# Routing made ready during attention, top-2 choice per batch, and identity products between the logits

## The chip, the cores and the metric

The kernel runs on one core of one Trainium2 chip. Its time is device microseconds (us) of one execution. The kernel before the change takes 1905.55 us, the median of 3 runs (1905.47 to 1907.82).

## The reference, cut to what matters

Four blocks add to a residual `x` of 4 batches x 1024 tokens x 256 channels: attention over a context, a mixture of experts, a second attention, and a second mixture of experts. What the change touches is the routing of both mixtures:

```python
x = x + attention0(layernorm(x), ctx)
x = x + ffn0(layernorm(x))        # 8 experts, hidden 1024, top 2
x = x + attention1(layernorm(x), ctx)
x = x + ffn1(layernorm(x))        # 8 experts, hidden 512, top 2
# in each ffn:
logits = z @ router               # z: normalised tokens, 8 logits per token
probs = softmax(logits)
top_w, top_idx = top_k(probs, 2)
w = top_w / (sum(top_w) + 1e-9)
out = sum over the 2 chosen experts of w * expert(z)
```

The reference computes all experts for every token; the kernel computes only the two chosen ones, so it must first sort the 8192 (token, choice) pairs by expert.

## The kernel before, in words

A token tile is 128 tokens, one per partition; there are T = 32 tiles, TB = 8 per batch. The program is a row of blocks, each with one instruction stream per engine; a block starts on all engines when all of them have ended the one before. The order is written out by hand: every engine runs its list in order and waits on counters. The blocks are `attention0_inputs`, `attention0`, `route` (layer 0), `experts` (layer 0), `attention1_context`, `attention1`, `route` (layer 1), `experts` (layer 1).

`route` (line 800) has three stages.

1. **The turning loop.** `summarise` (line 306) turns the per-token sums that attention left in `g.stats` into mean and variance for all 32 tiles, on DVE; POOL raises the variance to the power -1/2 (line 877), 4 columns first and then 28. DVE's `center` (line 972) writes the normalised tile into one of R = 4 slots of `z`. PE transposes it in two halves (`turn`, line 896), ACT copies the result to SBUF (`copy_out`, line 932) and writes a float16 copy of z (`token_high`, line 937), DVE the float16 remainder (`token_low`, line 977), which frees the slot. PE multiplies the transposed tile with the 8-column router weight `gw` (`logits`, line 902). SP stores the halves to `token_parts` in DRAM batch by batch, and between them brings five experts' weights (`bring_home`). `gw` itself is loaded at the start of the block, and PE waits for it before its first instruction (line 889).
2. **The choice.** After the last tile DVE works on all 32 tiles x 8 experts = 256 columns: each instruction increments `v_step` and DVE waits for it (`step`, line 994). It copies the logits, finds the best and the second best expert (lines 1005 to 1012), adds the two one-hot rows (line 1014); PE multiplies that with a strictly upper triangular matrix (ranks inside a tile, line 915) and with ones (totals of each tile, line 916); DVE runs 8 prefix sums over the tiles (line 1028) and computes each pair's slot, lane and block. ACT's exponentials (line 943) give the shares.
3. **The inverse permutation.** For 8 sets of 8 columns DVE builds one-hot rows of the block times token and times share (`same_block`, line 1072, then lines 1084 and 1086), and ACT (lines 953, 959; even sets) or DVE (line 1075; odd sets) the one-hot rows of the lane; PE multiplies them (line 923, 8 float32 products of 156 columns a set, two records each in the trace) and sums in one PSUM bank. `block_hot` and `lane_hot` have two buffers. In the loop from line 1079 DVE issues `same_block(i + 1)` before the two products of set i; `same_block(n)` waits until PE has read set n - 2.

At the end the slots' tokens and weights are read from PSUM (lines 1093, 1094), and `experts` starts by gathering rows from `token_parts`.

In `attention1` (line 1509) body c of each engine works on tile c in a pipeline: POOL's two passes over the 128x1232 scores (lines 1696, 1700), PE's transposes of them (line 1601), DVE's sums; the last batch drains over six bodies.

## Time and profile before

| | |
|---|---|
| median of 3 runs | 1905.55 us (1905.47 to 1907.82) |
| the profiled execution's own time | 1910.07 us |
| its span, first to last instruction | 1908.4 us |
| mean granted TensorE clock | 0.909 of full |
| PE / PEld busy | 1610.3 us (84%) / 1188.1 us (62%) |
| DVE / ACT / POOL busy | 1101.4 (58%) / 854.0 (45%) / 712.3 us (37%) |
| DMA | mean 84 GB/s |
| `route`, layer 0 | 573.5 to 690.9 us of the span |
| `route`, layer 1 | 1422.8 to 1538.8 us of the span |

PE is the matmul engine and PEld its weight loads. A busy share is an average over stages that have different limits. The granted clock is 1.00 at 2.4 GHz and 0.50 at 1.2 GHz. The times of the rows further down are counted from the span's first instruction. In the views by time, a bracket at the end of a row gives the engine's idle time before it and what ended that.

### The profile page before, as it was taken

The page shows a single profiled execution, that of the slowest core. Times are in us where ns is not written, and L with a number is a line of the kernel's source. Part 1 is how long each engine was busy: PE and PEld are TensorE (multiplying, and loading weights), DVE is VectorE, ACT ScalarE, POOL GpSimd, SP SyncE. Part 2 cuts the span into 40 slices and gives each one's busy share as a digit, 9 for nine tenths or more (in the row PEclk, how much of TensorE's full clock was granted, in tenths as well). Part 3 has the DMA queues.
Part 4 walks back from the last instruction along what each step waited for, and adds up shares of the span by engine and source line. Part 5 has one row for each costly group of instructions (what it writes and reads, how often), then busy time and mean ns, then how long its engine had stood idle before and what let it go on. Part 6 is the DMA issues. An engine that isn't in the chain of part 4 may idle for free. (4 is left out here: it accounts for less than half of the span.)

```text
span 1908.4 us, 38766 instructions
## 1 busy us (share of the span) xinstructions
PE 1610.3 (84%) x12456; PEld 1188.1 (62%) x12457; DVE 1101.4 (58%) x1819; ACT 854.0 (45%) x1506; POOL 712.3 (37%) x515
## 2 busy tenths in 40 slices
PE   4798898897987369999999994899968479999997
PEld 1433434334337358888888882677757468888886
DVE  4677677687676524445554431788857434444443
ACT  1663755655634215555554440466744312222221
POOL 2401302104001014655555441577760025556554
PEclk9899899899895679999999996799995689999999
DMA  4321320412307134555553221200016043333333
GB/s 127 105 67 45 110 66 25 129 44 77 100 22 271 59 141 128 141 140 135 132 132 66 47 42 37 83 24 22 24 56 221 0 133 59 62 56 58 63 55 45
DMA packets 104310, 159.84 MB, mean 84 GB/s; under 512 B 10810, under 2 KB 69998, under 8 KB 104110
## 3 DMA queue, kind: packets, MB, share of 16 engines
q1 hardware_dynamic: 73007, 117.52, 19.0%
q0 software_dynamic: 29952, 40.91, 12.3%
q8 instruction: 43, 0.70, 0.1%
q10 hardware_dynamic: 1279, 0.46, 0.1%
q14 instruction: 29, 0.24, 0.0%
HBM read 91.49 MB, written 67.37 MB: 83 GB/s over the span
## 5 line engine op out<-in xcount | busy, mean ns | idle before, releaser
L1234 PE MATMUL e_ph<-e_zTt,weights_a 128*128 128x256 f16 x3744 | 424.6, 274 | 32.5 <-issue 28.3
L1234 PEld LDWEIGHTS e_ph<-e_zTt,weights_a 128*128 x3744 | 360.6, 98 | 96.1 <-issue 53.1
L1188 POOL DMA_INDIRECT e_zt<-token_parts,slot_token x156 | 167.1, 1071 | 271.4 <-issue 263.4
L1319 ACT ACTIVATE e_h<-e_ph,e_b 128x256 f32<-128x256 f32 x312 | 131.0, 471 | 240.0 <-PE e_ph L1234 162.6
L1367 DVE TENSOR_TENSOR e_hl<-e_h,e_hh 128x512 f16<-128x512 f32 x156 | 104.7, 692 | 226.7 <-ACT e_hh L1333 202.1
L1198 POOL DMA_INDIRECT token_rows<-e_ysb,slot_token x78 | 151.7, 1945 | 200.1 <-DVE e_ysb L1384 185.7
L1248 PE MATMUL e_pyt<-weights_b,e_hh 128*128 x1248 | 210.7, 273 | 1.1 <-DVE e_ysb L1384 1.1
L640 ACT ACTIVATE probs<-lower_banks,shift 128x1024 f32<-128x1024 f32 x128 | 137.7, 1111 | 118.8 <-PE lower_banks L500 113.8
L1198 POOL DMA_INDIRECT out_dram<-e_ysb,slot_token x78 | 124.5, 1596 | 133.9 <-DVE e_ysb L1388 110.5
L1248 PE MATMUL e_pyt<-weights_b,e_hl 128*128 x624 | 170.1, 273 | 0.0
L1358 DVE SCALAR_TENSOR_TENSOR e_g<-e_ph,e_h 128x512 f32<-128x512 f32 x78 | 54.0, 692 | 178.1 <-PE e_ph L1234 171.3
L660 DVE TENSOR_TENSOR acc<-acc,probs 128x1024 f32<-128x1024 f32 (+1 forms) x112 | 136.9, 1222 | 28.3 <-ACT probs L640 25.2
L511 PE MATMUL middle_banks<-probs,v 128*64 128x512 f32 (+1 forms) x576 | 142.6, 606 | 1.0 <-ACT probs L640 1.0
L500 PE MATMUL lower_banks<-qT,kT 128*128 128x512 f16 x512 | 131.2, 401 | 4.7 <-ACT kT L606 4.7
L1248 PEld LDWEIGHTS e_pyt<-weights_b,e_hh 128*128 128x128 f16 x1248 | 122.1, 98 | 15.1 <-issue 1.3
L1322 ACT ACTIVATE e_h<-e_ph 128x512 f32<-128x512 f32 x78 | 46.6, 598 | 170.5 <-PE e_ph L1234 159.6
L923 PE MATMUL e_pinv<-e_block_hot,e_lane_hot 128*128 128x156 f32 x256 | 61.5, 425 | 64.2 <-DVE e_block_hot L1086 64.2
L500 PEld LDWEIGHTS lower_banks<-qT,kT 128*128 128x128 f16 x512 | 46.8, 102 | 106.2 <-issue 33.4
L1248 PE MATMUL e_pyt<-weights,e_hh 128*128 x624 | 108.6, 273 | 0.5 <-DVE e_ysb L1388 0.5
L676 POOL COPY cshift<-shift 77x1 f32 x4 | 0.7, 184 | 278.2 <-PE middle_banks L468 278.2
L923 PEld LDWEIGHTS e_pinv<-e_block_hot,e_lane_hot 128*128 128x128 f32 x256 | 57.8, 295 | 68.9 <-issue 68.9
L1333 ACT CAST e_hh<-e_h 128x512 f16<-128x512 f32 x156 | 92.4, 620 | 0.0
(240 smaller groups left out, 2973.0 us busy)
## 6 DMA issues: line engine op xcount, KB each, us to landing
weight_parts<-w_split SPq DMA_DIRECT2D x32, 512.0 KB, 3.3
weights_a<-weight_parts SPq DMA_DIRECT2D x16, 1024.0 KB
x_sb<-in_u SPq DMA_DIRECT2D x24, 512.0 KB
weight_parts<-x_sb SPq DMA_DIRECT2D x24, 512.0 KB
w_raw<-in_w1T SPq DMA_DIRECT2D x16, 512.0 KB, 4.4
w_raw<-in_w2T SPq DMA_DIRECT2D x16, 512.0 KB, 4.7
weights_b<-weight_parts SPq DMA_DIRECT2D x8, 1024.0 KB
token_parts<-x_sb SPq DMA_DIRECT2D x8, 1024.0 KB, 5.3
```

The source lines that it names most:

```text
L500: last = pe.matmul(sc[0:rows(k), n % 2, j, :], kk, q, start=(form == 0), stop=(form == 1))
L511: last = pe.matmul(po[u % 2][j * HD0:(j + 1) * HD0, :], v[0:rows(k), k, h * HD0:(h + 1) * HD0], pr[0:rows(k), n % 4, j, :], start=(k == 0) ...
L640: act.activation(pr[0:r, n % 4], sc[0:r, n % 2], ACT.Exp, bias=bias).then_inc(e_done, 1)
L660: dve.tensor_tensor(acc[0:r, u % 2], acc[0:r, u % 2], pr[0:r, n % 4], ALU.add).then_inc(acc_done, 1)
L923: pe.matmul(pinv[:, 0:2 * NT * C], lane_hot[n % 2][:, w, :], block_hot[n % 2][:, w].rearrange("p h n -> p (h n)"), start=(c == 0), stop=(c ...
L1188: pool.indirect_dma_start(zt[:, i % 2, c, :], None, g.zrows, at).then_inc(ld[i % 2], 16)
L1198: pool.indirect_dma_start(g.rows[layer], at, ysb[:, s, c, :], None, compute_op=ALU.add).then_inc(sto[s], 16)
L1234: last = pe.matmul(ph[:, q, f, :], up_w(wp, e, k, 2 * q + f), zTs[:, s, 2 * zp + k, :], start=(n == 0), stop=(n == 5))
L1248: last = pe.matmul(py[c][:, 0, :], hp[:, s, f, c * P:(c + 1) * P], down_w(wp, e, f), start=(n == 0), stop=(n == 3 * NF - 1))
L1319: last = act.activation(h32[:, q % 2, f, :], ph[:, q, f, :], ACT.Relu, bias=b1[:, bass.ds(e, 1), 2 * q + f], scale=1.0 / WS)
L1333: act.copy(hh[:, s, 2 * q:2 * q + 2, :], src[:, q % 2]).then_inc(hi_done, 1)
L1367: dve.tensor_tensor(hl[:, s, 2 * q:2 * q + 2, :], src[:, q % 2], hh[:, s, 2 * q:2 * q + 2, :], ALU.subtract).then_inc(lo_done, 1)
```

## The change

- `gw` for both layers is loaded in `attention0` (`g.gw`); `route` no longer loads it or waits for it.
- The temporaries of `summarise` are shared, and it takes a range of tiles and a run number. Tiles 0 to 23 (LAST = 24) are summarised on DVE, and rooted on POOL by the new `roots`, inside the attentions: in `attention0` in the last batch after its projections, in `attention1` in body c = 15. `route` does tiles 24 to 31 only: DVE after its second `token_low`, POOL at the block's start, and DVE waits for that before `center(24)`.
- The choice is made batch by batch (`choose(b)`, 64 columns): for batches 0, 1, 2 inside the turning loop after `center` at t = 10, 18, 26, with ACT's exponentials at t = 12, 20, 28 (ACT waits there for `choose`) and the shares (`weigh(b)`) on DVE at t = 13, 21, 29. Only batch 3 comes after the loop. The logits have two PSUM banks, one for even and one for odd batches.
- The 8 prefix sums now run before PE's products, on the one-hot sums (line 1014's result); PE adds the ranks inside a tile and the counts of earlier tiles in one PSUM sum. DVE's copies of the totals and two 256-column additions go.
- In the third stage the two products of set i come before `same_block(i + 1)`.
- PE multiplies the identity by itself in float32 (128 columns, result unused): 12 times at the start of `route`, once between each `turn` and `logits`, and 36 times after the last logits.
- `attention1`'s SP waits for the store before last to have landed before each store of x.

```diff
+def roots(pool, g, run, t0, t1):
+    pool.wait_ge(g.stat_steps, 7 * run)
+    pool.tensor_tensor(g.rstd[:, t0:t1], g.stat_ve[:, t0:t1], g.neghalf[:, t0:t1], ALU.pow).then_inc(g.stat_roots, 1)
...
@@ attention0, SP @@
+            for i, gate in enumerate((a["routerT"], a["gate"])):
+                sp.dma_start(g.gw[:, i], gate.rearrange("(k p) e -> p k e", p=P)).then_inc(g.cleared, 16)
...
@@ attention0, DVE, after the projections of a batch @@
+                if not more:
+                    dve.wait_ge(st_done, LAST)
+                    summarise(dve, g, 2, 0, LAST, False)
...
@@ route, POOL and PE @@
-            pool.wait_ge(g.stat_steps, summed)
-            for t0, t1 in ((0, 4), (4, T)):
-                pool.tensor_tensor(g.rstd[:, t0:t1], stat_ve[:, t0:t1], g.neghalf[:, t0:t1], ALU.pow
-                                   ).then_inc(g.stat_roots, 1)
+            roots(pool, g, 3 + 2 * layer, LAST, T)
+            pool.memset(passed[:, 0, :], 0.0).then_inc(p_step, 1)
...
-            pe.wait_ge(ld, 16)
...
+            def keep_going(n):
+                for _ in range(n):
+                    pe.matmul(idle[:, 0:P], g.ident[:], g.ident[:], start=True, stop=True)
+            keep_going(12)
             turn(0)
             for t in range(1, T):
                 turn(t)
+                keep_going(1)
                 logits(t - 1)
             logits(T - 1)
-            pe.wait_ge(p_step, 7)
-            pe.wait_ge(v_step, CHOSEN)
-            sel = z[:, 1, :]
-            pe.matmul(prk[:, 0:T * E], upper[:], sel, start=True, stop=True)
-            pe.matmul(ptot[:, 0:T * E], g.ones[:], sel, start=True, stop=True).then_inc(rk_done, 1)
+            keep_going(36)
+            pe.wait_ge(p_step, 8)
+            pe.wait_ge(chosen, B)
+            pe.matmul(prk[:, 0:T * E], upper[:], lane_hot[0][:, 2:4, :].rearrange("p w n -> p (w n)"), start=True, stop=False)
+            pe.wait_ge(scanned, E)
+            pe.matmul(prk[:, 0:T * E], g.ones[:], passed[:, 0:T, :].rearrange("p t e -> p (t e)"), start=False, stop=True)
+            pe.matmul(ptot[:, 0:E], g.ones[:], passed[:, T, :], start=True, stop=True).then_inc(rk_done, 1)
...
@@ route, ACT @@
+            def exponentials(b):
+                ts = slice(b * TB, (b + 1) * TB)
+                act.wait_ge(shifted, b + 1)
+                act.activation(ex[:, ts, :], l2[:, ts, :], ACT.Exp).then_inc(ex_done, 1)
+                act.activation(e1[:, ts], sm[:, ts], ACT.Exp).then_inc(ex_done, 1)
             for t in range(T):
                 copy_out(t)
                 token_high(t)
-            act.wait_ge(v_step, SHIFTED)
-            act.activation(ex, l2[:], ACT.Exp).then_inc(ex_done, 1)
-            act.activation(e1[:], sm[:], ACT.Exp).then_inc(ex_done, 1)
-            act.wait_ge(p_step, 7)
-            act.wait_ge(v_step, LANES)
+                if t >= TB and t % TB == AFTER + 2:
+                    exponentials(t // TB - 1)
+            exponentials(B - 1)
...
@@ route, DVE @@
+            def choose(b):
+                ts = slice(b * TB, (b + 1) * TB)
+                dve.wait_ge(lg_done, (b + 1) * TB)
+                step(dve.tensor_copy(lg[:, ts, :].rearrange("p t e -> p (t e)"), plg[b % 2][:, 0:TB * E]))
+                for src, top, oh in ((lg, m0, oh0), (l2, m1, oh1)):
+                    step(dve.tensor_reduce(top[:, ts], src[:, ts, :], AX.X, ALU.max))
+                    step(dve.tensor_tensor(wk[:, ts, :], src[:, ts, :], over_e(top[:, ts], TB), ALU.is_equal))
+                    step(dve.tensor_tensor(wk2[:, ts, :], wk[:, ts, :], over_t(rev[:], TB), ALU.mult))
+                    step(dve.tensor_reduce(r0[:, ts], wk2[:, ts, :], AX.X, ALU.max))
+                    step(dve.tensor_tensor(oh[:, ts, :], over_t(rev[:], TB), over_e(r0[:, ts], TB), ALU.is_equal))
+                    if src is lg:
+                        step(dve.scalar_tensor_tensor(l2[:, ts, :], oh0[:, ts, :], MASKED, lg[:, ts, :],
+                                                      ALU.mult, ALU.add))
+                dve.tensor_tensor(wk[:, ts, :], oh0[:, ts, :], oh1[:, ts, :], ALU.add).then_inc(chosen, 1)
+                if b == B - 1:
+                    dve.wait_ge(chosen, B)
+                    for e in range(E):
+                        dve.tensor_tensor_scan(passed[:, 1:T + 1, e], g.ones[:, 0:T], wk[:, :, e], 0.0,
+                                               ALU.mult, ALU.add).then_inc(scanned, 1)
+                step(dve.tensor_tensor(l2[:, ts, :], lg[:, ts, :], over_e(m0[:, ts], TB), ALU.subtract))
+                dve.tensor_tensor(sm[:, ts], m1[:, ts], m0[:, ts], ALU.subtract).then_inc(shifted, 1)
+            def weigh(b):
+                ts = slice(b * TB, (b + 1) * TB)
+                dve.wait_ge(ex_done, 2 * b + 2)
+                step(dve.tensor_reduce(den[:, ts], ex[:, ts, :], AX.X, ALU.add))
+                step(dve.tensor_scalar(den[:, ts], den[:, ts], 1e-9, 1.0, ALU.mult, ALU.add))
+                step(dve.tensor_tensor(den[:, ts], den[:, ts], e1[:, ts], ALU.add))
+                step(dve.reciprocal(share[:, 0, ts], den[:, ts]))
+                step(dve.tensor_tensor(share[:, 1, ts], share[:, 0, ts], e1[:, ts], ALU.mult))
+            dve.wait_ge(g.stat_roots, 2 + 2 * layer)
             for t in range(R):
-                if t == 1:
-                    dve.wait_ge(g.stat_roots, roots + 2)
                 center(t)
             for t in range(T):
                 token_low(t)
                 if t + R < T:
                     dve.wait_ge(lo_done, t + 1)
+                    if t + R == LAST:
+                        dve.wait_ge(g.stat_roots, 3 + 2 * layer)
                     center(t + R)
...
+                if t == 1:
+                    summarise(dve, g, 3 + 2 * layer, LAST, T, False)
+                if t == 2:
+                    dve.wait_ge(p_step, 8)
+                if t >= TB and t % TB == AFTER:
+                    choose(t // TB - 1)
+                if t >= TB and t % TB == AFTER + 3:
+                    weigh(t // TB - 1)
+            choose(B - 1)
...
-            step(dve.tensor_reduce(den[:], ex, AX.X, ALU.add))
-            tot = ptot[:, 0:T * E].rearrange("p (t e) -> p t e", e=E)
-            step(dve.tensor_copy(ex, tot))
-            step(dve.tensor_scalar(wk2, ex, 0.0, 1.0, ALU.mult, ALU.add))
-            for e in range(E):
-                last = dve.tensor_tensor_scan(l2[:, :, e], wk2[:, :, e], ex[:, :, e], 0.0, ALU.mult, ALU.add)
-                n[0] += 1
-                last.then_inc(v_step, 1)
...
-            step(dve.tensor_tensor(l2[:], l2[:], ex, ALU.subtract))
-            step(dve.tensor_tensor(l2[:], l2[:], prk[:, 0:T * E].rearrange("p (t e) -> p t e", e=E), ALU.add))
-            step(dve.tensor_tensor(l2[:], l2[:], over_t(base[:]), ALU.add))
+            step(dve.tensor_tensor(lg[:], prk[:, 0:T * E].rearrange("p (t e) -> p t e", e=E), over_t(base[:]), ALU.add))
...
             for i in range(SETS):
-                if i + 1 < SETS:
-                    same_block(i + 1)
                 hot = block_hot[i % 2]
                 dve.wait_ge(same_done, i + 1)
                 dve.tensor_tensor(hot[:, :, 1, :], hot[:, :, 0, :], per_column(share, i, NT * C), ALU.mult
                                   ).then_inc(block_done, 1)
                 dve.tensor_tensor(hot[:, :, 0, :], hot[:, :, 0, :], per_column(token, i, NT * C), ALU.mult
                                   ).then_inc(block_done, 1)
+                if i + 1 < SETS:
+                    same_block(i + 1)
             step(dve.tensor_tensor(tiles[:], tiles[:], over_t(cumt[:], NT), ALU.is_ge))
...
@@ attention1, SP, POOL, DVE @@
+                sp.wait_ge(g.x_home, 16 * (B + b))
...
+                if c == SUMMARY:
+                    roots(pool, g, 4, 0, LAST)
...
+                if c == SUMMARY:
+                    dve.wait_ge(st_done, LAST)
+                    summarise(dve, g, 4, 0, LAST, False)
```

## Rows read from the trace of the kernel before

**Rows 1.** Busy time by stretch: us, each engine's busy us (instructions), clock, DMA, GB/s

```profile
573.50:618.50 45.00, 38.08 (x192) 37.59 (x192) 27.91 (x71) 21.70 (x64) 8.10 (x9) 0.53 0.79 273
618.50:640.70 22.20, 2.05 (x5) 1.17 (x4) 18.99 (x56) 6.60 (x19) 0.00 (x0) 0.50 0.45 151
640.70:690.90 50.20, 31.45 (x128) 29.85 (x128) 20.03 (x29) 8.36 (x19) 0.00 (x0) 0.72 0.00 1
...
1490.00:1538.80 48.80, 30.04 (x128) 27.93 (x128) 20.03 (x29) 8.36 (x19) 0.00 (x0) 0.75 0.00 0
```

**Rows 2.** PE by time in the turning loop (start, us, what)

```profile
595.21 0.67 PE L896 MATMUL e_pz<-ident,e_z 128*128 128x128 f32 x2
595.67 0.86 PE L902 MATMUL e_plg<-e_gw,e_zTs 128*128 128x8 f32 x4
```

**Rows 3.** Busy time by stretch, loop, gap, burst and attention 1

```profile
583.00:618.00 35.00, 35.00 (x180) 35.00 (x180) 23.90 (x58) 20.34 (x60) 0.00 (x0) 0.50 0.75 259
644.60:647.30 2.70, 0.33 (x3) 0.09 (x1) 2.25 (x3) 2.24 (x5) 0.00 (x0) 1.00 0.00 0
648.00:651.20 3.20, 3.20 (x13) 2.97 (x12) 0.00 (x0) 0.67 (x3) 0.00 (x0) 0.50 0.00 0
...
1240.00:1390.00 150.00, 141.25 (x1846) 116.93 (x1844) 133.00 (x232) 104.26 (x194) 115.50 (x70) 1.00 0.07 22
```

**Rows 4.** Groups of PE's instructions, 1240 to 1390 us

```profile
L1601 PE MATMUL pt<-ident,s 128*77 128x128 f32 x368 | 50.9, 281 | 8.7 <-ACT pT L1664 5.4 <-POOL s L1696 2.6
```

**Rows 5.** PE by time in attention 1, at clock 0.50 and at 1.00

```profile
1199.82 2.08 PE L1608 MATMUL front<-zT,wq 128*128 128x128 f32 x8 [0.46 <-ACT zT L1658]
...
1304.04 1.06 PE L1608 MATMUL front<-zT,wq 128*128 128x128 f32 x8
```

**Rows 6.** DVE by time, start of the turning loop

```profile
580.64 1.41 DVE L972 TENSOR_SCALAR e_z<-x_sb,mean,rstd 128x256 f32<-128x256 f32 x3 [4.36 <-POOL rstd L877]
581.97 0.42 DVE L977 TENSOR_TENSOR x_sb<-e_z,x_sb 128x256 f16<-128x256 f32 x1
...
582.75 0.42 DVE L977 TENSOR_TENSOR x_sb<-e_z,x_sb 128x256 f16<-128x256 f32 x1
```

**Rows 7.** DVE by time, the choice

```profile
618.54 0.42 DVE L1003 COPY e_r<-e_plg 128x256 f32<-128x256 f32 x1 [0.37 <-PE e_plg L902]
...
626.74 0.42 DVE L1023 TENSOR_REDUCE e_c<-e_z 128x32 f32<-128x256 f32 x1 [1.59 <-PE e_ptot L916]
...
627.98 1.10 DVE L1028 TENSOR_TENSOR_SCAN e_r<-e_z 128x32 f32<-128x32 f32 x8
...
634.24 0.23 DVE L1050 TENSOR_TENSOR e_s<-e_s 128x64 f32<-128x64 f32 x1
...
636.50 1.53 DVE L1072 TENSOR_TENSOR e_block_hot<-e_blocks,e_s 128x624 f32<-128x624 f32 x2
```

**Rows 8.** ACT by time, lane rows of the first even set

```profile
634.30 2.46 ACT L953 ACTIVATE e_apart<-e_lanes,e_s 128x128 f32<-128x128 f32 x8 [8.59 <-DVE e_s L1048]
```

**Rows 9.** PE, then DVE by time, the inverse permutation

```profile
647.36 4.00 PE L923 MATMUL e_pinv<-e_block_hot,e_lane_hot 128*128 128x156 f32 x16 [2.43 <-DVE e_block_hot L1086]
...
651.40 0.81 DVE L1072 TENSOR_TENSOR e_block_hot<-e_blocks,e_s 128x624 f32<-128x624 f32 x1 [4.18 <-PE e_pinv L923]
652.12 1.22 DVE L1075 TENSOR_TENSOR e_lane_hot<-e_lanes,e_s 128x1024 f32<-128x1024 f32 x1
653.26 0.80 DVE L1084 TENSOR_TENSOR e_block_hot<-e_block_hot,e_s 128x624 f32<-128x624 f32 x1
```

**Rows 10.** POOL's roots in both routes: ns min/median/max, first and last start

```profile
L877 POOL TENSOR_TENSOR rstd<-e_stat_ve,neghalf x4: 1018/2912/4807, 574.8 to 1425.1; 128x4 f32<-128x4 f32 x2, 128x28 f32<-128x28 f32 x2
```

**Rows 11.** POOL, PE and DVE by time, drain of attention 1

```profile
1395.51 2.25 POOL L1696 TENSOR_TENSOR s<-s,rs 128x1232 f32<-128x1232 f32 x1 [2.07 <-DVE rs L1761]
...
1397.81 1.10 PE L1601 MATMUL pt<-ident,s 128*77 128x128 f32 x8 [0.34 <-POOL s L1696]
...
1390.36 1.44 DVE L1738 TENSOR_TENSOR s<-psc,bias 128x1232 f32<-128x1232 f32 x1 [1.24 <-PE psc L1635]
```

More of the change, by code:

```diff
@@ L303, in _, with summarise @@
             last.then_inc(kt_done, 1)
-def summarise(dve, g, tmp, ve, twice):
-    seen = g.stat_seen
-    g.stat_seen += 7
-    stats, steps = g.stats, g.stat_steps
+def summarise(dve, g, run, t0, t1, twice):
+    seen = 7 * (run - 1)
+    tmp, ve = g.stat_tmp[:, :, t0:t1], g.stat_ve[:, t0:t1]
+    stats, steps = g.stats[:, t0:t1, :], g.stat_steps
     dve.tensor_tensor(tmp[:, 0, :], stats[:, :, 1], stats[:, :, 4], ALU.add).then_inc(steps, 1)
@@ L1054, in _ @@
             step(dve.tensor_tensor(token[:], ids[:], low8[:], ALU.add))
[L1055 to L1059 removed]
+            weigh(B - 1)
             def per_column(x, n, width):
```

110 lines of the change are left out of this document (44 added, 66 removed).

## The prediction

> **What bounds the kernel now.** I read the slices of the page, then the busy times by stretch, then the engines by time inside `route`. The kernel is not bound by one engine: its two routing blocks are stretches of their own between attention and experts, 117 us and 116 us long, and nothing of the experts runs beside them. [rows 1] cut the first into three stages: 45.0 us of turning loop, 22.2 us of choice in which PE does 2 us of work, and 50.2 us of inverse permutation in which PE is busy 31.5 us and DVE 20.0 us, that is, they take turns. The second route has the same stages, the last 48.8 us.
>
> In the turning loop PE is busy all the time [rows 3], at a granted clock of 0.50. A tile takes 1.17 us: the next tile's transposes would start 1.17 us after 595.21 (0.67 and 0.86 overlap), because each of the six records, two transposes and four passes of the float32 logits, takes 0.2 us at this clock [rows 2]. In the third stage PE works 4.00 us on a set and waits 2.43 us before it, longer before an odd one by DVE's 1.14 us of odd lanes [rows 9], since `same_block(n + 1)`, which waits for PE, is queued on DVE ahead of the products that PE waits for. The clock reaches 1.00 as a burst ends and is back at 0.50 in the next burst: 1.00 in 644.6 to 647.3, when PE does 0.33 us of work, and 0.50 in 648.0 to 651.2, when it is busy throughout [rows 3].
>
> **The change part by part.** All times are for the profiled execution, span 1908.4 us.
>
> *Prices.* A float32 product of 128 columns is two records. In attention 1 eight such records take 2.08 us at 0.50 and 1.06 us at 1.00 [rows 5]; less the pipelined end of the last, that is 0.213 and 0.112 us a record, so 0.43 and 0.22 us for one identity product. A DVE step of 64 columns takes 0.23 to 0.26 us: from 634.24 to 636.50 are nine steps of 32 or 64 columns, 0.25 each [rows 7].
>
> *Start.* Before, DVE waited 4.36 us at 580.64 for the second root and PE for the router weight [rows 6]. Now 24 tiles are rooted in advance, DVE starts at 573.5 and PE's 12 identity products run until 576.2 at 1.00 (12 x 0.22 = 2.7 us) or 578.6 at 0.50 (12 x 0.43 = 5.1). I take 2.7 for the first route, whose first stage has a mean of 0.53 though its loop ran at 0.50, so that it started high [rows 1, 3], and 5.1, the dearer case, for the second.
>
> *Turning loop at clock 1.00.* PE per tile: 1.17/2 + 0.22 = 0.81; I take 0.85, for records that don't halve exactly. DVE per tile is 0.79 (581.97 to 582.75, where DVE wasn't waiting [rows 6]). So while the clock is up, the tile is 0.85 instead of 1.17.
>
> *The choice in the loop.* `choose(b)` is 15 instructions, 13 of them full steps of 64 columns: 15 x 0.24 = 3.6 us of DVE; `weigh(b)` is 5, 1.05 us. What is queued behind `choose(0)` on DVE is `token_low(11)` and `center(15)`, and ACT waits in front of `copy_out(13)` until the end of `choose(0)`. PE has two tiles of work in hand then (1.9 us), and can go on 0.8 us after the choice (two exponentials, one copy): it stands still about 3.6 + 0.8 - 1.9 = 2.5 us. That is the gap after which the clock is found at 0.50 in the third stage (2.43 us, [rows 9, 3]). So I expect the clock to go at the first `choose`, at t = 10.
>
> *Turning loop at clock 0.50.* The mixture of the loop kept PE busy 35.00 of 35 us and never raised the clock [rows 3]; with one product more per tile it is denser, but DVE-fed and half transposes and small logits still. I take it that it does not come back: 1.17 + 0.43 = 1.60 us a tile, and PE sets the pace, so that the later choices are hidden (8 tiles are 12.8 us, DVE's 8 x 0.79 + 4.65 = 11.0). The bounds: 0.85 and 1.60.
>
> *Sum of the first stage.* PE starts turning at 2.7; up to the first choice (turn 10 done, then 1.6 us of copy, halves and center) 8.5 + 1.6 = 10.1, so 12.8; + 4.4 until PE goes on = 17.2; then logits 13 and 14 and tiles 15 to 31, 17 x 1.60 + 1.7 = 28.9. Total 46.1 against 45.0: the stage loses 1.1 us, in the second route 3.5. If the clock is held, DVE decides: 3.7 to the first `token_low`, 32 x 0.79 + 3 x 4.65 + 1.2 = 40.5, total 44.2.
>
> *After the last logits.* Before: 618.54 to 626.74 until DVE has the totals (8.2), then 14.0 to the first product at 640.7 [rows 7, 1]. Now DVE needs 13 x 0.25 + 1.1 (the eight prefix sums, [rows 7]) = 4.4 us. But the 36 identity products stand in PE's queue ahead of the ranks: 15.4 us at 0.50, 8.1 at 1.00. Back to back they raise the clock as a burst of the third stage does, whose clock was up by the end of 4.0 us [rows 9, 3]; allowing 3 to 6 us for it gives 14 to 28 records at 0.213 and the rest of the 72 at 0.112, 9.5 to 10.9 us; I take 10.1. The three products after them add 1.3: 11.4, a loss of 3.2. Then DVE: 14.0 less den, copy, factor and eight sums (626.74 to 629.1, 2.4), less two additions (0.9), less `same_block(1)` and the odd lanes, now behind the products (1.9), leaves 8.7, `weigh(3)` taking the place of four steps. ACT's lanes are ready (2.46 + 1.15 us after the lanes are known, 0.6 before they are needed, [rows 8]). 11.4 + 8.7 = 20.1 against 22.2: 2.1 us won.
>
> *Inverse permutation.* DVE's preparation of a set is 0.72 + 2 x 0.72 = 2.2 us (by starts, [rows 9]), with odd lanes 3.3, mean 2.75, and now runs beside PE's previous set. PE's set is 4.2 us at 0.50 and 2.1 at 1.00. PE has been idle 8.7 us, so sets 0 and 1 begin at 0.50; then there is no gap left until the clock rises, and from there DVE paces with gaps of PE of 0.1 to 1.2 us, shorter than any that lost the clock. Sum: sets 0 and 1, 6.9 us (4.2 + 2.7, clock rising on the way); 3.3 + 2.2 + 3.3 + 2.2 + 3.3 = 14.3 for the preparations 3 to 7; last set 2.1; reading the result 0.7: 24.0 instead of 50.2 and 48.8 [rows 1]. Gain 26.2 and 24.8. Bounds: all at 0.50, 8 x 4.2 + 0.7 = 34.3; DVE alone, 8 x 2.75 + 0.7 = 22.7.
>
> *What is moved into the attentions.* `summarise` is 1.2 us on DVE. In attention 0 DVE waits for the exponentials behind it: 0. In attention 1 DVE stood 1.24 us before the 1390.36 row [rows 11]: 0 to 1.2, I take 0. POOL's root of 24 columns: 4.8 us for 28 and 1.0 for 4 [rows 10], so 4.1. In body 15 POOL stood 2.07 us before 1395.51 [rows 11], so its pass starts 2.0 us later, PE's transposes at 1397.81 were waiting for that pass, and in the drain each later body hangs on PE's chain: 2.0 us lost (0 to 4.1). In attention 0 POOL is done by then. The router weights (2 x 8 KB) and SP's new waits, for stores that landed a batch ago: 0.
>
> *DMA.* It is busy 0.79 of the first stage and 0.45 of the second, and idle in the third [rows 1]; it stays hidden unless `route` gets shorter than some 57 us.
>
> Sum: first route -1.1 + 2.1 + 26.2 = 27.2; second -3.5 + 2.1 + 24.8 = 23.4; attention 1 -2.0. Together 48.6 us: span 1860 us. The profiled execution took 1910.07 us and the median is 1905.55; the same gain from the median gives **1857 us**.
>
> **A rule weighed.** Attention 1 holds clock 1.00 for 150 us with PE busy 141 of them [rows 3], 50.9 us of that in transposes of the scores alone [rows 4]. The Trainium skill, "TensorE: Matmul & The Clock Gate", "Part 4: PE-mode transpose", says that full clock does not engage for transposes, which don't count as busy in the same way. By that rule the loop, half of it transposes, would lose the clock at once; the trace of attention 1 speaks against it, though its other products could be what holds it. What it would cost is the second rival.
>
> **The rivals.**
> 1. *The clock is held through the loop* (PE's pause at a choice is shorter than worked out). First stage 44.2 instead of 46.1, and the 36 products and three behind them take 9.0 us instead of 11.4: 4.3 us less a route, 1848 us. For it: the gap of 2.5 us is worked out, not seen. Against: 2.43 us was enough in every burst of the third stage.
> 2. *The clock is lost as soon as the loop begins.* 15 tiles at 1.60 instead of 0.85, 11 us a route. 1879 us. For it: the old loop stayed at 0.50 although PE was busy. Against: [rows 3, 4].
> 3. *The clock stays at 0.50 in the whole of `route`*, and the 79 identity products stand as plain work in PE's queue (34 us a route). 5.1 + 51.2 + 0.9 = 57.2 to the last logits (+12.2), 15.4 + 2.3 = 17.7 to the totals (+9.5), 8.7 (-5.3), 34.3 (-15.9 and -14.5): +0.5 and +1.9, with attention's 2.0 makes 1910 us, slower. It decides once neither 36 products nor gapless sets raise the clock. Against: every 4 us burst of the third stage raised it.
> 4. *The change doesn't do what it says*: PE and DVE still take turns in the third stage, as `same_block(n)` waits for set n - 2. Then some 1900 us. The order read in the code excludes it nearly.
>
> **How the numbers follow.** Forecast 0.74 (1857, by itself 1848 to 1866), rival 1 0.11, rival 2 0.09, rival 3 0.04, rival 4 0.02. The range leaves out the last two and the far ends: 1842 to 1879. What a measurement tells from no change is 0.2%, 3.8 us. Faster: all but rival 3 and a trace of 4, 0.95; same 0.02; slower 0.03.
>
> **What would show it.** The third stage 23 us long with DVE busy nearly all of it: right; 33 us with PE busy all along: the clock did not rise. The clock in the loop 1.00 up to about 15 us after the block's start and 0.50 from there: right; 0.50 from the start: rival 2; 1.00 to the end: rival 1. Between the last logits and the ranks, PE busy without a gap for 9 to 11 us while DVE waits 5 to 6 us. In attention 1, POOL's root in body 15 and the last residual 2 us later. The prediction is wrong if the third stage stays over 30 us or the loop takes over 50 us.

## The result and the profile after

The changed kernel takes **1872.6 us** (median of 4 runs, 1872.07 to 1874.3) against 1906.1 (4 runs, 1905.47 to 1907.82) of the kernel before beside it: ratio 0.9824, 95% interval 0.9807 to 0.9842, 33.5 us faster. Forecast were 1857 us, in a range of 1842 to 1879, and a gain of 48.6 us: the sign is right, the size 15 us too large. The profiled execution took 1872.07 us, its span is 1870.4 us, its mean clock 0.925 (before 0.909).

Busy time by stretch, first the three stages of the first route, then those of the second (us; busy us and instructions of PE, PEld, DVE, ACT, POOL; granted clock; DMA share; GB/s). They answer to [rows 1]:

```profile
571.40:623.60 52.20, 49.27 (x279) 49.00 (x279) 37.65 (x131) 22.26 (x70) 3.81 (x9) 0.59 0.69 240
623.60:644.40 20.80, 11.74 (x80) 11.58 (x80) 12.50 (x51) 5.08 (x15) 0.00 (x0) 0.75 0.44 152
644.40:669.60 25.20, 20.83 (x128) 19.51 (x128) 21.77 (x31) 9.65 (x24) 0.00 (x0) 0.90 0.00 1
...
1404.50:1455.60 51.10, 48.10 (x278) 47.85 (x279) 37.51 (x131) 22.39 (x70) 3.82 (x9) 0.62 0.61 207
1455.60:1476.80 21.20, 12.14 (x80) 11.98 (x80) 12.47 (x51) 5.06 (x15) 0.00 (x0) 0.74 0.36 124
1476.80:1502.30 25.50, 21.05 (x128) 19.74 (x128) 21.83 (x31) 9.68 (x24) 0.00 (x0) 0.90 0.00 1
```

The third stage is halved, 25.2 us for 50.2 in the first route and 25.5 for 48.8 in the second, and DVE is busy 21.8 us of it. The second is 1.4 us shorter, though PE does 10 us more in it. The first is longer, 52.2 us for 45.0. A route takes 98.2 and 97.8 us instead of 117.4 and 116.0 us.

PE by time in the third stage (start, duration, what, and in brackets the idle time before it and what ended it) answers to [rows 9]:

```profile
644.38 6.85 PE L944 MATMUL e_pinv<-e_block_hot,e_lane_hot 128*128 128x156 f32 x32 [9.06 <-DVE e_block_hot L1113]
651.43 2.36 PE L944 MATMUL e_pinv<-e_block_hot,e_lane_hot 128*128 128x156 f32 x16 [0.20 <-DVE e_block_hot L1113]
654.79 4.64 PE L944 MATMUL e_pinv<-e_block_hot,e_lane_hot 128*128 128x156 f32 x32 [1.01 <-DVE e_block_hot L1113]
660.72 4.64 PE L944 MATMUL e_pinv<-e_block_hot,e_lane_hot 128*128 128x156 f32 x32 [1.28 <-DVE e_block_hot L1113]
666.64 2.36 PE L944 MATMUL e_pinv<-e_block_hot,e_lane_hot 128*128 128x156 f32 x16 [1.28 <-DVE e_block_hot L1113]
```

A set is 16 records. The first two take 3.4 us each while the clock rises, the others 2.36, and PE waits at most 1.28 us for DVE where it waited 2.43 and more.

What the forecast did not have stands at the start of the loop. POOL, DVE and PE by time:

```profile
577.95 1.74 POOL L329 TENSOR_TENSOR rstd<-stat_ve,neghalf 128x8 f32<-128x8 f32 x1 [90.20 <-DVE stat_ve L323]
...
581.56 0.20 POOL L896 IOTA e_ids<- 128x64 f32 x1
581.79 0.43 DVE L1004 TENSOR_TENSOR x_sb<-e_z,x_sb 128x256 f16<-128x256 f32 x1 [3.14 <-POOL e_ids L896]
...
582.72 0.69 PE L905 MATMUL e_pz<-ident,e_z 128*128 128x128 f32 x2 [2.90 <-DVE e_z L999]
```

`dve.wait_ge(p_step, 8)` now stands behind step 2 of DVE's loop. POOL's list begins with the root of the last 8 tiles, which has to wait for a DVE summary at step 1; then come a fill, a mask and six iotas. DVE stands still for 3.14 us and PE for 2.90, and there, not at the first choice, the clock goes (the second route has the same two pauses, 3.15 and 2.91 us, and its clock goes 1.3 us behind PE's):

```profile
571.40:581.00 9.60, 8.39 (x74) 8.12 (x74) 4.54 (x17) 4.64 (x14) 3.05 (x7) 1.00 0.93 317
581.00:623.60 42.60, 40.88 (x205) 40.88 (x205) 33.11 (x114) 17.62 (x56) 0.76 (x3) 0.50 0.63 223
628.70:639.00 10.30, 6.61 (x56) 6.42 (x55) 3.27 (x12) 0.26 (x2) 0.00 (x0) 1.00 0.42 168
639.00:649.20 10.20, 4.83 (x19) 4.86 (x20) 8.33 (x21) 6.27 (x18) 0.00 (x0) 0.50 0.00 0
649.20:669.60 20.40, 16.03 (x111) 14.71 (x110) 18.35 (x27) 8.11 (x19) 0.00 (x0) 1.00 0.00 1
```

PE by time: one tile at clock 1.00 (the next transposes start 0.85 us later), one at 0.50 (1.60 us later), and the 36 products behind the loop (72 records), which answer to [rows 2]; then DVE's wait for them:

```profile
577.15 0.41 PE L905 MATMUL e_pz<-ident,e_z 128*128 128x128 f32 x2
...
577.63 0.51 PE L914 MATMUL e_plg<-gate_rows,e_zTs 128*128 128x8 f32 x4
578.00 0.41 PE L905 MATMUL e_pz<-ident,e_z 128*128 128x128 f32 x2
...
585.94 0.67 PE L905 MATMUL e_pz<-ident,e_z 128*128 128x128 f32 x2
586.40 0.63 PE L921 MATMUL e_idle<-ident 128*128 128x128 f32 x2
...
587.54 0.67 PE L905 MATMUL e_pz<-ident,e_z 128*128 128x128 f32 x2
...
623.60 10.73 PE L921 MATMUL e_idle<-ident 128*128 128x128 f32 x72
...
635.35 0.17 DVE L1069 TENSOR_SCALAR e_ei<-e_ptot 128x8 int32<-128x8 f32 x1 [6.78 <-PE e_ptot L937]
```

Last, the drain of attention 1, DVE, POOL and PE by time (compare [rows 11]):

```profile
1367.04 0.19 DVE L315 TENSOR_TENSOR stat_tmp<-stats 128x24 f32<-128x24 f32 x1
1367.26 2.12 DVE L317 TENSOR_SCALAR mean<-stat_tmp 128x24 f32<-128x24 f32 x1
1369.30 0.17 DVE L318 TENSOR_TENSOR stat_tmp<-stat_tmp 128x24 f32<-128x24 f32 x1
1369.50 2.12 DVE L320 SCALAR_TENSOR_TENSOR stat_tmp<-stat_tmp 128x24 f32<-128x24 f32 x1
...
1366.74 2.60 POOL L1724 TENSOR_TENSOR s<-s,rs 128x1232 f32<-128x1232 f32 x1 [1.20 <-DVE rs L1792]
1369.31 2.27 POOL L1728 TENSOR_TENSOR s<-s,mx 128x1232 f32<-128x1232 f32 x1
1371.91 4.18 POOL L329 TENSOR_TENSOR rstd<-stat_ve,neghalf 128x24 f32<-128x24 f32 x1 [0.33 <-DVE stat_ve L323]
1376.88 2.25 POOL L1724 TENSOR_TENSOR s<-s,rs 128x1232 f32<-128x1232 f32 x1 [0.79 <-DVE rs L1792]
...
1379.18 3.37 PE L1627 MATMUL pt<-ident,s 128*77 128x128 f32 x16 [2.75 <-POOL s L1724]
```

The summary takes 4.9 us of DVE instead of 1.2: two of its seven steps last until a running POOL pass ends. The root costs the 4.1 us that were forecast, but POOL then still waits 0.79 us for DVE before its next pass: DVE, late by its summary, is what holds that pass, 10.1 us after the last one's start, where the kernel before has 6.5. PE stands still for 2.75 us until the pass is done, where it waited 0.34 [rows 11], and its clock is 0.50 from 1379.7 to 1383.1; the kernel before has 1.00 in the whole drain. From the end of the first route to the start of the second are 734.9 us instead of 731.9: 3.0 lost, forecast 2.0.

### The profile page after: what moved, and what is told of

It is laid out like the page before. It is cut to its first block and busy times, and to the rows that moved or that the text cites. A ratio compares the mean times of both kernels' runs of the same rounds, so it can differ in the third digit from the quotient of the medians.

```text
span 1870.4 us, 39556 instructions
## 1 busy us (share of the span) xinstructions
PE 1632.1 (87%) x12776; PEld 1212.1 (65%) x12777; DVE 1116.3 (60%) x1945; ACT 853.8 (46%) x1518; POOL 704.9 (38%) x517
## 3 DMA queue, kind: packets, MB, share of 16 engines
q1 hardware_dynamic: 73007, 117.52, 19.2%
## 5 line engine op out<-in xcount | busy, mean ns | idle before, releaser
L1258 PEld LDWEIGHTS e_ph<-e_zTt,weights_a 128*128 x3744 | 359.9, 98 | 93.8 <-issue 49.6
L1212 POOL DMA_INDIRECT e_zt<-token_parts,slot_token x156 | 163.3, 1047 | 233.2 <-issue 221.1
L667 DVE TENSOR_TENSOR acc<-acc,probs 128x1024 f32<-128x1024 f32 (+1 forms) x112 | 136.9, 1222 | 28.4 <-ACT probs L647 25.3
L1724 POOL TENSOR_TENSOR s<-s,rs 128x1232 f32<-128x1232 f32 x32 | 72.7, 2273 | 51.7 <-DVE rs L1792 51.5
L1357 ACT CAST e_hh<-e_g 128x512 f16<-128x512 f32 x78 | 48.2, 618 | 83.5 <-DVE e_g L1382 83.5
```

Of the source, the lines that this page charges most:

```text
L667: dve.tensor_tensor(acc[0:r, u % 2], acc[0:r, u % 2], pr[0:r, n % 4], ALU.add).then_inc(acc_done, 1)
L1212: pool.indirect_dma_start(zt[:, i % 2, c, :], None, g.zrows, at).then_inc(ld[i % 2], 16)
L1258: last = pe.matmul(ph[:, q, f, :], up_w(wp, e, k, 2 * q + f), zTs[:, s, 2 * zp + k, :], start=(n == 0), stop=(n == 5))
L1357: act.copy(hh[:, s, 2 * q:2 * q + 2, :], src[:, q % 2]).then_inc(hi_done, 1)
L1724: pool.tensor_tensor(s[:, i], s[:, i], per_key(rs[:, i, :]), ALU.mult).then_inc(n_done, 1)
```

## The experiments

Theory: the gain is the third stage's and comes from the order of its queue on DVE. The identity products and the wait for POOL cost time in the other stages. Rival: the identity products keep or raise the clock and are part of the gain. The kernel before took 1907.3 to 1907.7 us beside them. The lengths of the routes are differences of start times in each trace; numbers in the text count the runs as they stand here.

| us | first route | second route | time |
|---|---|---|---|
| before | 117.4 | 116.0 | 1907.3 |
| changed | 98.2 | 97.8 | 1872.6 |
| order alone | 91.1 | 90.7 | 1857.0 |
| changed, order undone | 124.8 | 124.0 | 1927.8 |
| POOL first | 91.9 | 91.0 | 1859.4 |
| POOL first, products before turns | 92.2 | 93.6 | 1863.9 |
| no product in the loop | 91.7 | 91.0 | 1860.1 |
| no burst | 92.2 | 93.0 | 1860.2 |
| late summary | 98.2 | 97.7 | 1870.8 |
| no identity product | 84.4 | 84.1 | 1846.3 |
| all four edits | 82.0 | 83.4 | 1835.3 |
| all four, weights once | 81.7 | 81.7 | 1835.9 |
| clock held | 81.9 | 81.6 | 1835.6 |
| held, weights once | 78.7 | 79.9 | 1829.4 |

**1. The order alone**, on the kernel before:

```diff
             for i in range(SETS):
-                if i + 1 < SETS:
-                    same_block(i + 1)
                 hot = block_hot[i % 2]
...
+                if i + 1 < SETS:
+                    same_block(i + 1)
```

> The kernel before with one part of the change alone: in the third stage the two products of set i are queued on DVE ahead of `same_block(i + 1)`. Theory: this is the whole of the gain. The third stages take 25 us instead of 50.2 and 48.8, with the clock risen to 1.00 by the second set; total 1906 - 49 = 1857 us, below the changed kernel, so that the rest of the change costs about 15 us. Rival: without the burst of identity products PE is cold for longer and the clock stays at 0.50 in the third stage: 34 us each, total about 1875.

1857.0 us, ratio 0.974 (0.9724 to 0.9757): the theory's time (50.3 us less than the kernel before beside it, where the theory had 49), and 15.6 us faster than the changed kernel. PE by time:

```profile
639.30 9.41 PE L923 MATMUL e_pinv<-e_block_hot,e_lane_hot 128*128 128x156 f32 x48 [12.37 <-DVE e_block_hot L1084]
650.03 4.64 PE L923 MATMUL e_pinv<-e_block_hot,e_lane_hot 128*128 128x156 f32 x32 [1.31 <-DVE e_block_hot L1084]
```

Here no burst goes before, PE has been idle for 12.37 us, and still the first three sets take 9.41 us and the rest 4.64 a pair, as in the changed kernel. The third stage raises its clock by itself.

**2. All but the order**, the same lines swapped back in the changed kernel.

> The changed kernel with the order of the third stage as before: `same_block(i + 1)` ahead of the two products of set i. All else is as in the changed kernel. Theory: the gain is that order's. The third stages are 50 and 49 us again instead of 25.2 and 25.5, the first inverse product comes 1.9 us later: 26 us a route, total about 1925, which is slower than the kernel before. Rival: the identity products and the earlier choice are worth something by themselves: then at least not slower than before, 1906 or below.

1927.8 us, ratio 1.0108 (1.0091 to 1.0125), 2.8 above the theory. All the rest of the change by itself makes the kernel slower, by 20.1 us. PE's third stage has its old gaps again (2.43 and 3.56 us), although the burst preceded it:

```profile
652.01 4.03 PE L944 MATMUL e_pinv<-e_block_hot,e_lane_hot 128*128 128x156 f32 x16 [2.43 <-DVE e_block_hot L1115]
659.61 3.76 PE L944 MATMUL e_pinv<-e_block_hot,e_lane_hot 128*128 128x156 f32 x16 [3.56 <-DVE e_block_hot L1115]
```

The two halves, 50.3 won and 20.1 lost, make 30.2, against 33.5 together: they are nearly independent. The remaining runs take the 20 apart.

**3. POOL's constants first.**

```diff
-            roots(pool, g, 3 + 2 * layer, LAST, T)
             pool.memset(passed[:, 0, :], 0.0).then_inc(p_step, 1)
...
+            roots(pool, g, 3 + 2 * layer, LAST, T)
```

> The changed kernel with one edit: in `route`, POOL writes its constants (one fill, one mask, six iotas) first and takes the root of the last 8 tiles after them, so that DVE's wait behind turn 2 finds them ready. Theory: the part of the forecast gain that is missing in the first stage comes from that wait (3.1 us of DVE, 2.9 us of PE) and from the clock that falls there, at tile 7 instead of at the first choice at tile 10. The wait is gone and the clock is 1.00 until the first `choose`: start to last logits 46.5 us instead of 52.2 in the first route and about 46 instead of 51.0 in the second, 5 to 6 us a route, total about 1862 us. Rival: the clock falls at that place of its own, because half of the loop is transposes: then only the 3 us of the wait go, if they go, loop 49 us, total about 1867. A second rival, in which the wait is hidden anyway: 1872.6, no change.

1859.4 us, ratio 0.9748 (0.9732 to 0.9765): 13.2 us, where the theory had 10.6. Busy time by stretch of the first stage:

```profile
571.40:587.70 16.30, 14.74 (x134) 14.36 (x134) 13.44 (x45) 8.71 (x26) 4.07 (x9) 1.00 0.84 276
587.70:618.20 30.50, 29.08 (x145) 29.09 (x146) 24.24 (x87) 13.48 (x44) 0.00 (x0) 0.50 0.74 262
```

PE at the first choice, by time:

```profile
589.12 1.02 PE L914 MATMUL e_plg<-gate_rows,e_zTs 128*128 128x8 f32 x4 [2.95 <-ACT e_zTs L953]
```

This is the first stage of the forecast: 46.8 us (forecast 46.1), clock 1.00 up to the first choice, a pause of 2.95 us there (forecast 2.5), 0.50 from it on. The rivals, that the clock falls at PE's turn 7 of its own or that the wait is hidden, are out.

**4. No product in the loop** (`keep_going(1)` left out).

> The changed kernel without the one identity product between the logits; the 12 ahead of the loop and the 36 behind it stay. Theory: at clock 0.50 the product is plain work, 0.43 of the 1.60 us of a tile, and keeps no clock. Without it PE needs 1.17 us a tile and DVE sets the pace (0.79 a tile and 4.65 for a choice with its weights, 32 us for the last 23 tiles instead of 37.7): 5 us less in each loop, total about 1862 us. Rival: the product is what holds clock 1.00 in the first tiles and what lets the burst behind the loop raise it soon; without it the first tiles go at 0.50 too (7 tiles x 0.33 = 2.3 us) and the burst takes longer: 3 us a route given back, total about 1869.

1860.1 us, ratio 0.9754 (0.9738 to 0.977), 1.9 below the theory. First transposes to last logits take 6.0 us less in the first route (43.6 for 49.6) and 4.7 in the second. The rival is out on both counts: the clock is 1.00 until 581.4, as long as in the changed kernel, with PE through its first seven turns and 1.4 us into its pause; and the burst of 72 records behind it takes 10.32 us instead of 10.73, so it is not slower for what stands ahead.

**5. No burst** (`keep_going(36)` left out).

> The changed kernel without the 36 identity products behind the last logits. Theory: they only stand in PE's queue ahead of the ranks. DVE's scans are done 4.5 us after the last logits, then three products at clock 0.50 (2.4 us): totals 7 us after the last logits instead of 11.75 and 12.15, and the inverse permutation starts at 0.50 in both kernels, since PE is idle 9 us before it. 4.7 and 5.1 us less, total about 1863 us. Rival: the burst's clock is still of use in the third stage (it starts faster, 25.2 us instead of some 29): then 4 us a route are given back and the total is about 1871.

1860.2 us, ratio 0.9755 (0.9739 to 0.9771), 2.8 below the theory. Second and third stage:

```profile
624.80:639.90 15.10, 2.54 (x8) 1.74 (x7) 12.50 (x51) 5.08 (x15) 0.00 (x0) 0.50 0.60 208
639.90:664.60 24.70, 20.18 (x128) 18.87 (x128) 21.66 (x31) 9.65 (x24) 0.00 (x0) 0.93 0.00 1
```

Totals come 6.0 us behind the end of the last logits instead of 11.6 (11.75 from the burst's start), and the third stage is no longer for it. In the changed kernel the burst raised the clock to 1.00 for 10.3 us, from 628.7 to 639.0. DVE waited for the rest of the burst until 635.35 and worked alone behind it; when PE's sets began at 644.38 the clock was at 0.50 again.

**6. No identity product at all.**

> The changed kernel without any identity product: neither the 12 ahead of the loop, nor the one in each turn, nor the 36 behind it. Theory: they bring nothing anywhere; the loop is DVE's, the third stage starts at 0.50 in both kernels and rises in its own first 5 us. First stage 46 us from DVE's start (the wait for POOL still in it), totals 6 us behind it, first inverse product 9.0 later, inverse permutation 25.3: 86.5 us a route instead of 98, total 1849 us. Rival: together they do keep the clock up, and without the 12 ahead the first tiles run at 0.50 and the third stage takes 29 us: total about 1858.

1846.3 us, ratio 0.9678 (0.9662 to 0.9694): 2.7 us below the theory. The rival was right on the clock, which is 0.50 from 576.2 on, PE's fourth turn, and wrong on its price: the third stage takes 25.3 us. The first stage is 44.1 us, not 46: a part of DVE's wait for POOL now lies behind PE's slower tiles. PE's 79 extra products cost 26 us in two routes.

**7. The summary late in attention 1.**

```diff
-    SUMMARY = TB + LAG + 3
+    SUMMARY = 2 * TB + 2
+    ROOTS = 2 * TB + 3
...
-                if c == SUMMARY:
+                if c == ROOTS:
                     roots(pool, g, 4, 0, LAST)
```

> The changed kernel with the 24-tile summary in attention 1 moved to where POOL and DVE have nothing left to do: DVE's summary from body 15 to body 18, POOL's root of 24 columns behind its last pass, in body 19. Theory: the summary in body 15 holds up the drain of attention 1 by 3 us (DVE's two 24-column steps of 2.12 us beside POOL's passes, then POOL's root of 4.18 us ahead of the next pass); POOL is idle for the last 8 us of attention 1, so that the root is free there. Between the routes 731.8 us instead of 735.0, total 1869.4 us. Rival: the drain hangs on PE's chain only, and what is not lost in body 15 is lost at the start of the second route, which waits for the root: 1872.6, no change.

1870.8 us, ratio 0.9809 (0.9793 to 0.9825). The times alone, 1.9 us apart, don't settle it; the traces do: 731.7 us between the routes instead of 734.9, the 3.2 of the theory. POOL by time:

```profile
1384.68 2.29 POOL L1725 TENSOR_TENSOR s<-s,rs 128x1232 f32<-128x1232 f32 x1 [0.23 <-DVE rs L1793]
...
1393.06 4.18 POOL L329 TENSOR_TENSOR rstd<-stat_ve,neghalf 128x24 f32<-128x24 f32 x1
```

DVE by time at its summary:

```profile
1384.89 2.12 DVE L317 TENSOR_SCALAR mean<-stat_tmp 128x24 f32<-128x24 f32 x1
1386.92 0.17 DVE L318 TENSOR_TENSOR stat_tmp<-stat_tmp 128x24 f32<-128x24 f32 x1
1387.12 0.18 DVE L320 SCALAR_TENSOR_TENSOR stat_tmp<-stat_tmp 128x24 f32<-128x24 f32 x1
```

The root now ends at 1397.2 and the route begins at 1401.1. The `TENSOR_SCALAR` again lasts until POOL's pass ends (1386.97); the `SCALAR_TENSOR_TENSOR` behind it, with POOL idle, takes 0.18 us instead of 2.12.

**8. All four edits** (POOL first, no identity products, summary late).

> The changed kernel with all four edits: POOL's constants first, no identity products, the 24-tile summary late. Theory: the terms add up, since each is a piece of its own on the path: 3.1 us a route for POOL's wait on top of the kernel without identity products, and 3.2 us in attention 1: total 1849 - 6.2 - 3.2 = 1840 us. Rival: without identity products PE turns at clock 0.50 from the start and is the bound of the loop as before, so that POOL's wait is hidden behind PE (32 x 1.17 = 37.4 us and the pauses at the choices): then 1846.

1835.3 us, ratio 0.9625 (0.9609 to 0.9641): 37 us below the changed kernel. The sum said 1840, the rival 1846. Both were partly right on the loop: with PE at 1.17 us a tile, POOL's wait was worth 1.9 us a route (44.1 and 44.3 down to 42.1 and 42.5), not 3.1. Against run 6 the span is 11.8 us shorter: 3.3 in the routes, 5.1 between them, where 3.2 were expected, and 3.4 outside, ahead of the first route for the most part, where the two kernels are the same. That start moves by itself: among the kernels that are the same up to there the first route begins anywhere from 570.5 to 573.9 us of the span. Between the routes the seven traces with the early summary have 734.9 to 736.3 us, the five with the late one 730.8 to 731.7; the clock of 0.50 in the drain is in all of the first and in none of the second. The median is 11.0 shorter. Busy time by stage:

```profile
570.60:612.70 42.10, 38.00 (x192) 36.20 (x192) 37.59 (x131) 22.00 (x70) 4.16 (x9) 0.53 0.86 297
612.70:627.80 15.10, 2.55 (x7) 1.69 (x7) 12.46 (x51) 5.04 (x15) 0.00 (x0) 0.50 0.62 209
627.80:652.60 24.80, 20.21 (x128) 18.90 (x128) 21.75 (x31) 9.70 (x24) 0.00 (x0) 0.93 0.00 1
```

Run 8 is also 21.7 us faster than run 1, which has the order and nothing else. So what is left of the change when its products, its wait and its early summary are gone, that is the roots taken ahead, the choice in the loop and the shorter second stage, is worth some 22 us; no run tells these parts from each other. In run 2 they were there too, and their gain was hidden under what the rest cost.

**9. What is the clock worth in the loop?** First, ten products before turns 15, 23 and 31, on top of run 3:

```diff
             for t in range(1, T):
+                if t >= TB + 7 and t % TB == 7:
+                    keep_going(10)
                 turn(t)
```

> Compared with the kernel in which POOL's constants come first (1859.4): ten more identity products in front of turns 15, 23 and 31, where PE stands still for a choice. Theory of the forecast: the clock is lost because PE pauses for the choice, so with the pause filled it stays at 1.00 through the loop; then DVE sets the pace, the first stage is 3.7 + 32 x 0.79 + 3 x 4.65 = 43 us from DVE's start instead of 46.8, the burst behind it runs at 1.00 (9 us to the totals instead of 11): 5 to 6 us a route, total about 1849. Rival: the clock is lost in this loop whatever fills the pauses, since half of its work is transposes; then 30 products of 0.43 us stand in PE's queue, which sets the pace there: up to 13 us a route, 8 us after what DVE hides, total about 1875.

1863.9 us, ratio 0.9775 (0.9759 to 0.9791): neither 1849 nor 1875. PE by time shows why:

```profile
588.75 1.02 PE L914 MATMUL e_plg<-gate_rows,e_zTs 128*128 128x8 f32 x4 [2.98 <-ACT e_zTs L955]
589.62 4.61 PE L921 MATMUL e_idle<-ident 128*128 128x128 f32 x20
594.03 0.45 PE L905 MATMUL e_pz<-ident,e_z 128*128 128x128 f32 x2
```

My products stood behind the pause, not in it: PE's queue stops at logits 13, ahead of turn 15. They brought the clock back (1.00 from 594.2) and cost their own time. So the run is a failed test of the pause, and a good one of the rival in it: the clock then stayed at 1.00 for 10.2 us, until behind the next pause of 2.29 us, in a loop with two transposes a tile.

Then with the products ahead of the logits that wait, without the burst, and with the other edits of run 8:

```diff
                 turn(t)
-                keep_going(1)
+                keep_going(11 if t >= TB + 6 and t % TB == 6 else 1)
                 logits(t - 1)
```

> Compared with the kernel that has all four edits (1835.3): the 12 products ahead of the loop and the one in each turn are back, and eleven instead of one stand in front of logits 13, 21 and 29, at which PE waits for a choice, so that they run inside the pause and not behind it. No burst behind the loop. Theory: the clock stays at 1.00 from the start of the route to the last logits, and it is worth almost nothing: with the tile at 0.84 DVE sets the pace (0.79 a tile, 14 us for three choices and weights), the loop takes 41 to 43 us from DVE's start, as in the kernel without any identity product (42.1); the totals come 5 us behind it instead of 6: total 1833 to 1837. Rival: full clock is worth what it seems, 32 tiles x (1.17 - 0.84) = 10 us a route, less what is already hidden: total about 1822.

1835.6 us, ratio 0.9619 (0.9603 to 0.9635), as in run 8 (0.9625). Busy time in the first stage:

```profile
571.50:613.10 41.60, 37.77 (x338) 36.74 (x338) 36.64 (x130) 22.00 (x70) 4.07 (x9) 1.00 0.85 291
```

PE by time in the filled pause:

```profile
585.92 2.62 PE L921 MATMUL e_idle<-ident 128*128 128x128 f32 x22
589.26 0.61 PE L914 MATMUL e_plg<-gate_rows,e_zTs 128*128 128x8 f32 x4 [0.72 <-ACT e_zTs L952]
```

The clock is 1.00 for the whole loop, where it is 0.53 on average in run 8, and the loop is 41.6 us instead of 42.1. Full clock was to be had, and with the products that it takes it is worth half a microsecond: DVE sets the pace as soon as PE doesn't. Beside run 3, whose loop has the 12 products and the one in each turn but loses the clock at the first choice, it is 5.2 us (41.6 for 46.8): the held clock pays for the products, and hardly more.

**10. The weights once**, for 32 tiles behind the last choice, in place of four times (first on top of run 8):

```diff
-                if t >= TB and t % TB == AFTER + 3:
-                    weigh(t // TB - 1)
             choose(B - 1)
+            weigh()
```

> Compared with the kernel that has all four edits (1835.3): the weights are worked out once, for 32 tiles, behind the last choice, instead of three times in the loop (1.05 us each) and once ahead of the inverse permutation. Theory: the loop's bound there is PE at 1.17 us a tile with three pauses of 1.2 us, so that the DVE time taken out of the loop is worth nothing, and only the weigh that stood between the totals and the first inverse product goes (1.1 us, of which 0.4 comes back, since the one weigh has to be done before DVE looks at the totals): 0.7 us a route, total about 1834. Rival: DVE sets the pace of the loop (37 of its 41.6 us busy): then 3.1 us a route more are won, total about 1828.

1835.9 us, ratio 0.9622 (0.9606 to 0.9638), no change: the loop took 42.1 us as before, with DVE busy 35.4 us instead of 37.6. And on top of the held clock:

> The last two together: clock held at 1.00 through the loop, and the weights worked out once. Theory: PE's bound (1.17 us a tile) and DVE's (0.79 and the choices with weights) lie close together, so that either edit by itself brings little and both bring what DVE saves in the loop: 3.1 us a route for the loop, 0.7 and 1 behind it, total 1835.3 - 9 = 1826. Rival: with the clock held PE's identity products take what is saved, or the clock is lost at the shorter loop's pauses: total as the better of the two, about 1834.

**1829.4 us**, ratio 0.9592 (0.9576 to 0.9608), first stage 39.4 us: the fastest kernel of the case, 78 us below before and 43 below the changed one. Either edit alone is worth nothing, both together 6 us. The sum said 9; the traces give 3.2 and 1.7 us in the routes, beside the run with the clock held.

## Why the prediction was right or wrong

*Inverse permutation*: right. 25.2 and 25.5 us where 24.0 were forecast, by the mechanism named, DVE's preparation beside PE's sets; runs 1 and 2 give the gain to the order alone.

*Totals to the first inverse product*: 9.0 us (forecast 8.7; its terms make 8.8). *After the last logits*: 11.6 and 12.0 us to the totals (forecast 11.4), DVE waiting 6.8 and 7.2 for the burst. Both right; run 5 shows the burst to be pure loss.

*Turning loop*: the prices were right (0.84 and 1.60 us a tile, forecast 0.85 and 1.60; `choose` 3.56 us, forecast 3.6). The step that failed is "So I expect the clock to go at the first `choose`, at t = 10." It went at PE's turn 7, because the list of what DVE waits for left out `dve.wait_ge(p_step, 8)`. The diff has it in plain sight, and POOL's eight constants and its root had no row in the prediction. It cost 2.9 us of pause and 0.76 us on each of seven tiles more, less 2.5 for the pause at the choice, which slower tiles then hid: 5.7 of the 6.1 us that the first stage ran over. With that wait gone (run 3) the stage is 46.8 us and the kernel 1859.4. The second route's stage ran over by 2.6 us only, mainly since its start was priced at 5.1 us and took 2.8. That the clock, once lost, would not come back in the loop was right: 0.50 for 42.6 us, with PE busy 40.9 of them.

*Attention 1*: the root's 4.1 us were right, the path was not. DVE's summary, put at 0 (0 to 1.2 us), took 4.9, and it is DVE that the next pass of POOL waited for, 0.79 us behind the root's end. The pass came 3.6 us late, not 2.0, and PE's clock fell in the gap that this made, which has no term in the forecast. 3.0 us lost for 2.0. Run 7 moved summary and root together, so what the root alone would have cost stays open.

The sum by terms: the routes gained 19.2 and 18.2 us instead of 27.2 and 23.4, attention lost 3.0 instead of 2.0; that makes 34.4, and the medians say 33.5. (The spans differ by 38.0; 3.6 of these lie ahead of the first route, 2.1, and behind the second, 1.5. Ahead of it the change only adds work, and the start moves by up to 3.4 us between traces of the same code, see run 8; so I don't count them as gain.)

The sign and the wide range came true. The narrow one, 1848 to 1866 for the forecast by itself, did not, and neither did one of its own signs: the loop was to stay under 50 us, and the first stages took 52.2 and 51.1 us (from the first transposes to the last logits 49.6 and 48.4). The time lies between the forecast and rival 2, because the clock went between the two places that they name. And the 57 us of DMA do not follow from the rows: 0.79 of 45.0 us and 0.45 of 22.2 us are 45.5 us.

*The rivals.* Rival 2 (clock lost as the loop begins) and rival 3 (0.50 throughout) are refuted by the clock of 1.00 in 571.40 to 581.00 and in the third stage. Rival 1 is refuted as it stood: PE's pause at the first choice was 2.95 us, and the clock went there (run 3). That the clock can be held with other products was shown by run 9. Of the rival's 4.3 us a route 1.9 were for the first stage; it took 41.6 us there, not 44.2. The other 2.4, for a burst at full clock, no run measured. Rival 4 is refuted by run 1.

*The rule weighed.* The prediction calls the loop half transposes; in the kernel before they are two of four products a tile, and two of its six records. What the traces show is that it matters whether the clock is up already. Once it is down, the loop does not raise it: not in the kernel before (0.50 for 35.0 us with PE busy throughout [rows 3]), and not with an identity product in each turn either (changed kernel, second route: 0.50 from 1417.2 to 1455.6, PE busy 38.4 of 38.4 us). While it is up the loop keeps it, with the identity product (run 9's second kernel, 41.6 us, in which PE never paused for more than 1.1 us) and without it (run 4, PE's first seven turns). The pauses inside the loop with which it went were 2.3 to 3.2 us long, though one of 2.30 in run 9's first kernel left it up. What raised it in or behind the loop were identity products back to back, ten and 36 of them. The Trainium skill, "TensorE: Matmul & The Clock Gate", "Part 4: PE-mode transpose", says that full clock does not engage for transposes because they don't count as busy in the same way. The trace agrees so far as this loop never raised the clock by itself; whether the transposes or the 8-column products are what doesn't count, no run here tells apart.

The prediction also did not ask what the identity products would be worth if they did what they seem to be for. They made PE faster beside a DVE that was as busy (38.0 and 37.6 of 42.1 us in run 8), and stood in the queue of the work that they were to speed up.

## What to carry to other kernels

- Split a large change by stage and ask of each part whether it pays alone. Here two lines of queue order gained 50 us, and all the rest together lost 20, though a part of that rest was worth some 22 by itself (run 8 beside run 1); the sum looked like a success.
- When a wait moves ahead in a queue, list everything that its releaser has to do first, in order, from the other engine's queue. A pause of 3 us cost as much again by the clock that went with it.
- Work that is there to keep a clock up pays only where that engine is the bound by more than the next one, and only if it runs inside the pause; behind the last wait it delays what everybody waits for. Two bounds that lie close together have to be moved together.

## What the hardware showed that I had not expected

A DVE instruction of 24 columns can take 2.12 us instead of 0.18. In two traces the float32 `TENSOR_SCALAR`, and once the `SCALAR_TENSOR_TENSOR`, ended within 0.1 us of the end of a POOL pass that was running as they began; with POOL idle they took 0.18. POOL's pass, in turn, took 2.60 us instead of 2.25 where three DVE `TENSOR_TENSOR` with two inputs ran in the first half microsecond of its record (from 1366.81), each in its usual 0.19. The Trainium skill, "SBUF — State Buffer", "SBUF: two separate sides", describes a port pair shared by the two engines as an exclusive lock that the first to start holds for its whole instruction, for DVE instructions with two SBUF inputs or in a mode that uses both ports. The traces agree for DVE, though that the one-input `TENSOR_SCALAR` ran in such a mode is not shown; for POOL, whose record would have to begin before it holds the ports, the one row only fits.

A root on POOL costs by the column: 1.74 us for 8 columns, 4.18 for 24, and 1.0 and 4.8 for 4 and 28 [rows 10].
